# Attention stage: rotations moved behind the score maxima, the choice matmuls moved into a scores bank, both heads' turned probabilities copied at once

## The chip, the cores and the metric

One core of one Trainium2 chip runs one fused program. The metric is the device time of the whole program in microseconds (us). The engines work in parallel, each through its own list of instructions in order: TensorE (PE, whose weight loads are listed as PEld), VectorE (DVE), ScalarE (ACT), GpSimd (POOL) and SyncE (SP, which only starts transfers). They meet at semaphores, which the program sets and waits for by hand. No scheduler reorders anything: what stands in an engine's list is what that engine does next, and a wait holds up all that stands behind it on its engine.

## The reference

Three layers over x of 8 batches x 256 tokens x 128:

```python
    x = x + 0.5 * _L0_ffn_ref(_layernorm(x, axis=-1), ...)
    x = x + _L0_attn_ref(_layernorm(x, axis=-1), ...)
    x = x + 0.5 * _L0_ffn_ref(_layernorm(x, axis=-1), ...)
```

The first and third are the same mixture of 64 experts (each token's 8 best, and a shared one). The one between is attention, 16 heads of 64:

```python
        q = q * cos + rotate_half(q) * sin + fenc
        k = k * cos + rotate_half(k) * sin + fenc
        dots = jnp.einsum('bhid,bhjd->bhij', q, k) * scale
        attn = jax.nn.softmax(dots, axis=-1)
        out = jnp.einsum('bhij,bhjd->bhid', attn, v)
        out = out.transpose(0, 2, 1, 3).reshape(b, n, INNER)
        return out @ w_out.T + b_out
```

## The kernel before

The change is in `attention`, the middle stage. It works in units of one batch and one pair of heads: 8 batches (`BATCH`) x 8 pairs (`PAIRS`) = 64 units, u = 8b + p. Batches 2 to 6 run in a loop on most engines; the others are written out.

The steps of a unit are spread over several turns of the loop over p. In the turn (b, p) the engines work on different units at once:

- **Projections** `qkv` (L72, L73, L74: three matmuls for one product of split float32): q and k of unit u+3 (`AHEAD` = 3) into bank `QB`, six matmuls of 128x256; v of unit u+3 into the first half of bank `VB`, three matmuls.
- **Rotation** `rotate` on DVE (L2076 with cos, L2079 with sin): from `QB` into the buffers `m1` and `m2`. POOL adds the two (`add`, L1856, 128x512 float32, SBUF to SBUF). PE turns the sum (`turn`, L1947, and two matmuls of the Fourier part, L1952) and ACT copies it out (`take_qk`, L2257).
- **Scores** (`scores`, L1962) of unit u into banks `SB` and `SB+1`, one for each head. They contract over 64 rows, so the two heads use half the rows of the array each.
- **Softmax**: `maximum` on DVE (L2086) for each head, `exps` on ACT (L2263) with the sums of rows; `invert` on DVE (L2092, 128x2). Head 0 is normalised on DVE (`normalise`, L2098, two instructions of 128x256, SBUF to SBUF), head 1 on ACT (L2272).
- `turn_p` (L1974) transposes the probabilities of unit u-1, into banks `PB` and `PB+1`; ACT copies each head's (`take_p`, L2279) into `pT`. `values` (L1987) of unit u-2 (`VLAG` = 2), 64 columns of the array for each head, into the second half of `VB`; ACT copies that (`take_o`, L2284). `project` (L2002) of unit u-3 (`JLAG` = 3). `take_v` (L2246) copies v out of the first half of `VB`.

Bank `VB` is shared: `values` waits until v of unit u+2 has been copied out (`vev`), and the v product waits until the values of unit u-2 have been copied out (`oev`).

Beside this, DVE adds up the first layer's choices for a later batch (`choice`, L2108, two instructions a turn, both inputs in SBUF), makes the layer norm of the next batch (`stats`, `mean`, `apply`, `split`, `bias`), and does most of the choice of experts for the third layer from the batch that is done (`pick_...`). Three times a batch (p = 0, 5, 6) a choice step needs the array and a bank: `pick_ranks`, `pick_turn`, `pick_logits` write into `room`, the first half of `VB`, and ACT takes the result at the head of the turn. From batch 2 on POOL sends two indirect transfers (`dispatch`, L1181) each turn.

Of the kernel before, what the change touches and what calls it, by code (L numbers as in the profile page):

```python
# [26 lines left out]
P = 128  # L27
BATCH, SEQ, DIM = 8, 256, 128
# [1715 lines left out]
def attention(nc, x, wk, ydram, attn_w, ready_w, y01, y01_in, summed, s, ps, wg, tables, xs_dram, sents):  # L1744
# [10 lines left out]
    with ExitStack() as ctx:  # L1755
# [62 lines left out]
        LN_STATS, LN_MEAN, LN_APPLY, LN_BIAS = 0, 1, 2, 3  # L1818
# [5 lines left out]
        with nc.Block(no_gpsimd_drain=True) as block:  # L1824
# [14 lines left out]
            def _(pool):  # L1839
# [3 lines left out]
                def load_cur(b):  # L1843
                    after(pool, vp, PAIRS * b)
# [23 lines left out]
                def batch(b):  # L1868
                    last = b == BATCH - 1
                    for p in range(PAIRS):  # L1870
                        if there(b, p, -AHEAD, False, last):
                            add(*pair(b, p, AHEAD))
# [43 lines left out]
            def _(pe):  # L1916
                def qkv(b, p, xs):
# [6 lines left out]
                    mm.then_inc(qk, 1)  # L1924
                    taken = u - AHEAD - VLAG + 1
# [42 lines left out]
                def turn_p(b, p, h):  # L1968
                    u = PAIRS * b + p
                    pe.wait_ge(pn[h], u + 1)  # L1970
                    after(pe, pte, 2 * u + h - 1)
# [35 lines left out]
                def room(b, p):  # L2007
                    u = PAIRS * b + p
                    pe.wait_ge(vev, min(u + AHEAD, PAIRS * BATCH) if isinstance(u, int) else u + AHEAD)
                    pe.wait_ge(oev, u - VLAG)  # L2010
                    return ps[:, VB, 0:TPB * P]

                def batch(b, kind):
                    first, last = kind == FIRST, kind == LAST
                    for p in range(PAIRS):
                        scores(b, p)
                        if p == 0 and kind in (MIDDLE, LAST):
# [5 lines left out]
                        if there(b, p, -1, first, last):  # L2023
                            turn(*pair(b, p, 1))
                        if there(b, p, 1, first, last):
                            turn_p(*earlier(b, p, 1), 0)
                            turn_p(*earlier(b, p, 1), 1)
                        if p == 0 and kind in (MIDDLE, LAST):
                            pe.wait_ge(s.room_r, 3 * (b - 2) + 3)
                        if p == PICK_TURN and not first:  # L2030
                            pe.wait_ge(s.room_r, 3 * (b - 1) + 1)
                        if p == PICK_LOGITS and not first:
                            pe.wait_ge(s.room_r, 3 * (b - 1) + 2)
                        if there(b, p, VLAG, first, last):
                            values(*earlier(b, p, VLAG), last and p + AHEAD > PAIRS)
                        if p + AHEAD < PAIRS:
                            qkv(b, p + AHEAD, xcur)
                        elif not last:
                            if p + AHEAD == PAIRS:
                                pe.wait_ge(xx, b + 2)  # L2040
                            qkv(b + 1, p + AHEAD - PAIRS, xnext)
                        if there(b, p, JLAG, first, last):
                            project(*earlier(b, p, JLAG), not last, last and p + AHEAD >= PAIRS)
                        if p == LN_TURN and not last:
                            turn_x(b + 1, False)
# [5 lines left out]
                qkv(0, 0, xnext)  # L2051
                qkv(0, 1, xnext)
                turn(0, 0)
                qkv(0, 2, xnext)
# [17 lines left out]
            def _(v):  # L2072
# [80 lines left out]
                def split(b):  # L2153
                    v.wait_ge(xev, b + 1)
                    after(v, vp, PAIRS * (b - 1) + AHEAD)
# [20 lines left out]
                def batch(b, kind, more):  # L2176
                    first, last = kind == FIRST, kind == LAST
                    for p in range(PAIRS):
                        maximum(b, p, 0)
                        maximum(b, p, 1)  # L2180
                        if p == RES_AT and not first:
                            residual(b - 1)
                        invert(b, p, 0)
# [29 lines left out]
                        if there(b, p, -AHEAD, first, last):  # L2213
# [277 lines left out]
```

## Time and profile before

| | |
|---|---|
| median of three runs | 913.99 us (912.68 to 914.81) |
| the profiled execution | 914.71 us, of which the span from first to last instruction is 912.7 us |
| PE, PEld busy | 93%, 82% of the span |
| DVE, ACT, POOL busy | 62%, 55%, 54% |
| attention stage | from about 294 us to 663 us |

A span is read by stage. Outside the attention stage the program is the two expert layers, where other things bind, and where the change alters nothing. In the attention stage one turn of the loop takes some 5.6 to 5.9 us, and 64 of them stand one behind the other. So an edit that makes a turn 0.1 us longer or shorter is worth about 6 us. Each row of the chain of waits or of the timeline has the start (us from the span's start) and the length of what it lists.

### The profile page before, as it was taken

How to read it: one execution, taken by the hardware profiler on the slowest of the kernel's cores; microseconds unless marked ns; L12 is line 12 of the kernel's file. 1: busy time of each engine (PE TensorE's matmuls, PEld its weight loads, DVE VectorE, ACT ScalarE, POOL GpSimd, SP SyncE). 2: the span in 40 equal slices, each digit the busy share in tenths (PEclk: the TensorE clock that was granted, in tenths of full speed). 3: DMA queues.
4: the chain of work that ended last, by engine and by line, in shares of the span. 5: the costliest groups of instructions: out<-in, count | busy, mean ns of one | idle time of the engine just before them, and what ended most of it. 6: DMA issues, size and time to landing. Idle time of an engine off the chain costs nothing.

```text
span 912.7 us, 18913 instructions
## 1 busy us (share of the span) xinstructions
PE 850.9 (93%) x6328; PEld 745.5 (82%) x6328; DVE 568.5 (62%) x1736; ACT 503.8 (55%) x1376; POOL 494.3 (54%) x536
## 2 busy tenths in 40 slices
PE   5989989999964999999999999999979999999977
PEld 4889989999963777777777777777679999999962
DVE  7947753333336878888888888877543376433446
ACT  4423333333321888888888888888832333333336
POOL 4156777777762222256666666666657354444440
PEclk9779999999995999999999999999999999999999
DMA  9947877776626890000000000000050588888756
GB/s 327 368 160 225 258 231 227 236 242 218 205 87 227 197 151 1 1 14 27 23 25 25 25 25 25 22 19 15 6 211 18 182 313 284 279 287 291 241 190 259
DMA packets 65150, 140.70 MB, mean 154 GB/s; under 512 B 10223, under 2 KB 37296, under 8 KB 63940
## 3 DMA queue, kind: packets, MB, share of 16 engines
q1 hardware_dynamic: 53316, 118.59, 39.9%
q0 software_dynamic: 11776, 21.39, 7.5%
q8 instruction: 31, 0.51, 0.2%
q14 instruction: 27, 0.22, 0.1%
HBM read 107.72 MB, written 35.56 MB: 157 GB/s over the span
## 4 chain that ended last, share of the span: by engine, by line
PE 62%; POOL 13%; issue 6%; DVE 5%; ACT 4%; DMA 4%; DVEq 0%; ACTq 0%; POOLq 0%; SPq 0%
PE ps L1387 12%; PE ps L1962 6%; POOL y_rows L589 6%; POOL f_xg L578 6%; PE ps L1987 6%; PE ps L1406 6%; PE ps L615 5%; PE ps L1974 5%; PE ps L72 4%; PE ps L1947 3%; PE ps L2002 3%; PE ps L73 2%; PE ps L74 2%; ACT at_prob L2263 2%; PE ps L655 2%
## 5 line engine op out<-in xcount | busy, mean ns | idle before, releaser
L1856 POOL TENSOR_TENSOR at_m<-at_m 128x512 f32<-128x512 f32 x64 | 81.5, 1274 | 147.8 <-DVE at_m L2079 147.8
L1181 POOL DMA_INDIRECT xs_rows<-xr,slots_of x128 | 127.4, 995 | 43.8 <-issue 32.1
L2263 ACT ACTIVATE at_prob<-ps,at_nmax 128x256 f32<-128x256 f32 x256 | 118.0, 475 | 39.2 <-DVE at_nmax L2086 38.8
L1365 POOL DMA_INDIRECT y_rows<-f_og,f_put x80 | 81.7, 1021 | 95.6 <-ACT f_og L1518 76.1
L878 DVE TENSOR_TENSOR f_ehid<-f_esil,ps 128x480 f32<-128x480 f32 (+1 forms) x80 | 50.8, 634 | 116.0 <-ACT f_esil L719 107.9
L1657 DVE TENSOR_TENSOR f_hid<-f_sil,ps 128x480 f32<-128x480 f32 (+1 forms) x80 | 50.7, 634 | 107.0 <-ACT f_sil L1511 100.4
L1387 PE MATMUL ps<-f_xgT,f_ring 128*128 128x160 f32 x768 | 115.0, 299 | 1.7 <-issue 1.7
L615 PE MATMUL ps<-f_xgT,f_ring 128*128 128x160 f32 x768 | 114.9, 299 | 0.2 <-issue 0.2
L719 ACT ACTIVATE f_esil<-ps 128x480 f32<-128x480 f32 (+1 forms) x80 | 44.4, 555 | 120.8 <-PE ps L615 120.8
L1511 ACT ACTIVATE f_sil<-ps 128x480 f32<-128x480 f32 (+1 forms) x80 | 44.4, 555 | 118.8 <-PE ps L1387 118.8
L1387 PEld LDWEIGHTS ps<-f_xgT,f_ring 128*128 128x128 f32 x768 | 107.0, 190 | 2.1 <-issue 2.1
L615 PEld LDWEIGHTS ps<-f_xgT,f_ring 128*128 128x128 f32 x768 | 107.0, 190 | 0.3 <-issue 0.3
L578 POOL DMA_INDIRECT f_xg<-xn_rows,f_take x80 | 84.0, 1050 | 34.1 <-issue 34.1
L2086 DVE TENSOR_REDUCE at_nmax<-ps 128x2 f32<-128x512 f32 x128 | 82.3, 685 | 25.0 <-PE ps L1962 24.6
L589 POOL DMA_INDIRECT y_rows<-f_og,f_put x80 | 79.7, 996 | 33.0 <-issue 23.5
L1962 PE MATMUL ps<-at_qkT 64*128 64x256 f32 x512 | 72.9, 403 | 2.1 <-ACT at_qkT L2257 2.1
L2279 ACT COPY at_pT<-ps 128x512 f32<-128x512 f32 x128 | 70.9, 627 | 0.0
L1987 PE MATMUL ps<-at_pT,at_v 128*64 128x256 f32 x512 | 69.4, 392 | 0.9 <-ACT at_pT L2279 0.9
L1974 PE MATMUL ps<-ident,at_prob 128*128 128x128 f32 x512 | 66.8, 273 | 1.3 <-ACT at_pT L2279 0.7
L655 PE MATMUL ps<-f_ehid,f_ring 128*128 128x160 f32 x384 | 62.6, 299 | 0.0
L1406 PE MATMUL ps<-f_hid,f_ring 128*128 128x160 f32 x384 | 62.6, 299 | 0.0
L2272 ACT ACTIVATE at_prob<-at_prob,at_rinv 128x256 f32<-128x256 f32 x128 | 61.2, 552 | 0.1
(256 smaller groups left out, 1844.2 us busy)
## 6 DMA issues: line engine op xcount, KB each, us to landing
f_ring<-in_wexp SPq DMA_DIRECT2D x128, 576.0 KB, 4.6
y_rows<-zeros SPq DMA_DIRECT2D x16, 512.0 KB, 6.2
f_yt<-y_rows SPq DMA_DIRECT2D x4, 2048.0 KB, 8.5
at_yt<-y_rows SPq DMA_DIRECT2D x6, 1024.0 KB, 4.9
xs_rows<-at_blank SPq DMA_DIRECT2D x16, 342.5 KB, 10.0
f_xg<-xs_rows SPq DMA_DIRECT2D x16, 342.5 KB, 3.3
y_rows<-f_og,f_put POOLq DMA_INDIRECT x160, 2.7
y<-y_rows SPq DMA_DIRECT2D x4, 512.0 KB, 4.4
```

Source lines behind the costliest of these rows:

```text
L578: nc.gpsimd.indirect_dma_start(xg[:, G % SG, c, :], None, xn_dram, bass.IndirectOffsetOnAxis(take[:, n:n + 1], 0), bounds_check=last_token ...
L589: nc.gpsimd.indirect_dma_start(ydram, bass.IndirectOffsetOnAxis(put[:, n:n + 1], 0), og[:, G % SG, c, :], None, bounds_check=last_row, oob ...
L615: mm = nc.tensor.matmul(ps[:, HB + 2 * h + half, f * w:(f + 1) * w], weights[:, half * FFN + f * P:half * FFN + (f + 1) * P], moving, star ...
L1181: nc.gpsimd.indirect_dma_start(xs_dram, bass.IndirectOffsetOnAxis(s.slots_of[:, t, k:k + 1], 0), s.xr[:, t, :], None, bounds_check=last_sl ...
L1365: nc.gpsimd.indirect_dma_start(ydram, bass.IndirectOffsetOnAxis(put[:, n:n + 1], 0), og[:, g, c, :], None, bounds_check=last_row, oob_is_e ...
L1387: mm = nc.tensor.matmul(ps[:, HB + 2 * h + half, f * w:(f + 1) * w], weights[:, half * FFN + f * P:half * FFN + (f + 1) * P], moving, star ...
L1406: mm = nc.tensor.matmul(ps[:, OB, 0:CAPACITY], ring[:, GE * g + e, c], hid[:, e % 2, f * CAPACITY:(f + 1) * CAPACITY], start=(f == 0), sto ...
L1962: mm = nc.tensor.matmul(ps[:, SB + h, t * SEQ:(t + 1) * SEQ], qkT[r, p % 2, t * P:(t + 1) * P], qkT[r, p % 2, SEQ:], start=True, stop=True)
L1974: mm = nc.tensor.transpose(ps[:, PB + h, j * SEQ + t * P:j * SEQ + (t + 1) * P], prob[:, p % 2, h, t, j * P:(j + 1) * P], ident[:, :])
L1987: mm = nc.tensor.matmul(ps[h * DH:(h + 1) * DH, VB, SEQ:], vsb[:, p, j, h * DH:(h + 1) * DH], pT[:, p % 2, h, j, :], start=(j == 0), stop= ...
L2086: nc.vector.tensor_reduce(nmax[:, p % 2, h, :], ps[:, SB + h, :].rearrange("p (t k) -> p t k", t=TPB), AX.X, ALU.max, negate=True).then_in ...
L2263: mm = nc.scalar.activation(prob[:, p % 2, h, t, :], ps[:, SB + h, t * SEQ:(t + 1) * SEQ], ACT.Exp, bias=nmax[:, p % 2, h, t:t + 1], accum ...
```

## The change

Seven edits in one, all in `attention`:

1. DVE: `rotate` no longer ends a turn. It stands behind the two `maximum` (and behind `residual`), in front of `invert` and `normalise` of head 0, and it handles the q and k that were projected in the turn before, so unit u+2 in the turn of u.
2. POOL: `add` follows it, unit u+2 in the turn of u.
3. PE: the order of a turn is now scores, values, turn, turn_p, project, turn_x, v product, choice matmuls, q/k product. Before it was scores, choice matmuls, turn, turn_p, values, q/k product, v product, project, turn_x.
4. PE: the choice matmuls write into bank `SB`, after the first head's exponentials have read it, and the next turn's scores wait until ACT has read the result.
5. ACT: the order of a turn is now exps, take_o, take_qk, take_p, the copy of a choice step, normalise, take_v.
6. ACT: `take_p` copies both heads in one instruction of 128x1024; before, one of 128x512 for each.
7. DVE: `bias` moves from p = 3 to p = 5. Some waits name `qk` in place of `vp`, since the q/k product is now the later one.

```diff
                 def room(b, p):
                     u = PAIRS * b + p
-                    pe.wait_ge(vev, min(u + AHEAD, PAIRS * BATCH) if isinstance(u, int) else u + AHEAD)
-                    pe.wait_ge(oev, u - VLAG)
-                    return ps[:, VB, 0:TPB * P]
+                    pe.wait_ge(ex, 2 * u + 1)
+                    return ps[:, SB, 0:TPB * P]
...
+                        if p == PICK_TURN + 1 and not first:
+                            pe.wait_ge(s.room_r, 3 * (b - 1) + 1)
...
                         scores(b, p)
+                        if there(b, p, VLAG, first, last):
+                            values(*earlier(b, p, VLAG), ending)
+                        if there(b, p, -1, first, last):
+                            turn(*pair(b, p, 1))
+                        if there(b, p, 1, first, last):
+                            turn_p(*earlier(b, p, 1), 0, ending)
+                            turn_p(*earlier(b, p, 1), 1, ending)
+                        if there(b, p, JLAG, first, last):
+                            project(*earlier(b, p, JLAG), not last, not there_is_v)
...
+                            project_v(*nxt, xs)
...
+                        if there_is_v:
+                            project_qk(*nxt, xs)
...
                         maximum(b, p, 1)
                         if p == RES_AT and not first:
                             residual(b - 1)
+                        if there(b, p, 1 - AHEAD, first, last) and not (first and p == 0):
+                            rotate(*pair(b, p, AHEAD - 1))
                         invert(b, p, 0)
                         normalise(b, p, 0)
...
-                        if there(b, p, -AHEAD, first, last):
-                            rotate(*pair(b, p, AHEAD))
...
-                def take_p(b, p, h):
+                def take_p(b, p):
                     u = PAIRS * b + p
-                    act.wait_ge(pt, 2 * u + h + 1)
-                    nc.scalar.copy(pT[:, p % 2, h, :, :].rearrange("p j q -> p (j q)"), ps[:, PB + h, :]).then_inc(pte, 1)
+                    act.wait_ge(pt, 2 * u + 2)
+                    nc.scalar.copy(pT[:, p % 2, :, :, :].rearrange("p h j q -> p (h j q)"),
+                                   ps[:, PB:PB + 2, :].rearrange("p h c -> p (h c)")).then_inc(pte, 2)
```

The order of DVE in the turn p = 2 of the looped batches, before (at_m is `m1`/`m2`, at_nmax the maxima, at_prob the probabilities, at_yt the first layer's results):

```order
L2086 TENSOR_REDUCE at_nmax<-ps 128x2
L2092 RECIPROCAL at_rinv<-at_rsum 128x2
L2098 TENSOR_SCALAR at_prob<-at_prob,at_rinv 128x256 x2
L2105 REGISTER_ALU
L2108 ISA
L2108 SCALAR_TENSOR_TENSOR x<-at_yt,wk,x 128x128
L2108 ISA
L2108 SCALAR_TENSOR_TENSOR x<-at_yt,wk,x 128x128
L2092 RECIPROCAL at_rinv<-at_rsum 128x2
L2148 TENSOR_SCALAR at_xn<-x,at_mv,at_st 128x128 x2
L2076 TENSOR_TENSOR at_m<-ps,cos 128x512
L2079 TENSOR_TENSOR at_m<-ps,sin 128x512
```

and the same turn of the changed kernel, whose lines are numbered 9 higher here:

```order
L2095 TENSOR_REDUCE at_nmax<-ps 128x2
L2084 REGISTER_ALU
L2085 TENSOR_TENSOR at_m<-ps,cos 128x512
L2088 TENSOR_TENSOR at_m<-ps,sin 128x512
L2101 RECIPROCAL at_rinv<-at_rsum 128x2
L2107 TENSOR_SCALAR at_prob<-at_prob,at_rinv 128x256 x2
L2114 REGISTER_ALU
L2117 ISA
L2117 SCALAR_TENSOR_TENSOR x<-at_yt,wk,x 128x128
L2117 ISA
L2117 SCALAR_TENSOR_TENSOR x<-at_yt,wk,x 128x128
L2101 RECIPROCAL at_rinv<-at_rsum 128x2
```

The two rotations went from behind the turn's other work to a place directly ahead of the first RECIPROCAL and the normalising of head 0.

PE in the turn p = 3 of batch 1, before, from the scores to the first projection:

```order
L1962 MATMUL ps<-at_qkT 128x256 [waits at_qkev]
L1962 MATMUL ps<-at_qkT 128x256 x3
L1947 MATMUL ps<-ident,at_m 128x128 [waits at_msum]
L1947 MATMUL ps<-ident,at_m 128x128 x3
L1952 MATMUL ps<-ffs,wfs 128x256 x2
L1974 MATMUL ps<-ident,at_prob 128x128 [waits at_pte,at_pn0]
L1974 MATMUL ps<-ident,at_prob 128x128 x3
L1974 MATMUL ps<-ident,at_prob 128x128 [waits at_pte,at_pn1]
L1974 MATMUL ps<-ident,at_prob 128x128 x3
L1987 MATMUL ps<-at_pT,at_v 64x256 [waits at_vev]
L1987 MATMUL ps<-at_pT,at_v 64x256 x3
```

and of the changed kernel (L1965 are the scores, L1991 the values, L1950 and L1978 the two turns):

```order
L1965 MATMUL ps<-at_qkT 128x256 [waits at_qkev]
L1965 MATMUL ps<-at_qkT 128x256 x3
L1991 MATMUL ps<-at_pT,at_v 64x256 [waits at_vev]
L1991 MATMUL ps<-at_pT,at_v 64x256 x3
L1950 MATMUL ps<-ident,at_m 128x128 [waits at_msum]
L1950 MATMUL ps<-ident,at_m 128x128 x3
L1955 MATMUL ps<-ffs,wfs 128x256 x2
L1978 MATMUL ps<-ident,at_prob 128x128 [waits at_pn0]
L1978 MATMUL ps<-ident,at_prob 128x128 x3
L1978 MATMUL ps<-ident,at_prob 128x128 [waits at_pn1]
L1978 MATMUL ps<-ident,at_prob 128x128 x3
```

The values stand directly behind the scores now, with their wait for ACT's last copy of the turn before (`vev`), and all the rest of PE's turn stands behind that wait.

## Rows read from the trace of the kernel before

**Rows 1.** Busy time by stretch: PE, PEld, DVE, ACT, POOL, clock, DMA share, GB/s

```profile
450.00:500.00 50.00, 49.76 (x390) 38.48 (x387) 42.63 (x134) 43.22 (x138) 30.71 (x33) 1.00 0.07 25
```

**Rows 2.** The chain of waits in order of time over one turn: start, us, what

```profile
332.17 1.06 PE ps L1962 x8
333.24 0.59 PE ps L1947 x4
...
334.94 1.01 PE ps L1987 x8
335.95 0.32 PE ps L72
336.26 0.12 PE ps L73
...
336.85 0.26 PE ps L72
...
337.35 0.45 PE ps L2002 x4
```

**Rows 3.** The timeline of the same turn

```profile
331.87 0.68 DVE L2079 TENSOR_TENSOR at_m<-ps,sin 128x512 f32<-128x512 f32 x1
...
332.10 1.14 PE L1962 MATMUL ps<-at_qkT 64*128 64x256 f32 x8
332.64 1.27 POOL L1856 TENSOR_TENSOR at_m<-at_m 128x512 f32<-128x512 f32 x1 [3.80 <-DVE at_m L2079]
332.67 0.42 ACT L2246 COPY at_v<-ps 128x256 f32<-128x256 f32 x1
...
333.27 1.29 DVE L2086 TENSOR_REDUCE at_nmax<-ps 128x2 f32<-128x512 f32 x2 [0.71 <-PE ps L1962]
...
335.05 0.17 DVE L2092 RECIPROCAL at_rinv<-at_rsum 128x2 f32<-128x2 f32 x1 [0.49 <-ACT at_prob L2263]
335.25 0.62 DVE L2098 TENSOR_SCALAR at_prob<-at_prob,at_rinv 128x256 f32<-128x256 f32 x2
...
336.27 0.40 ACT L2284 COPY at_oTh<-ps 128x256 f32<-128x256 f32 x1
336.31 0.16 DVE L2092 RECIPROCAL at_rinv<-at_rsum 128x2 f32<-128x2 f32 x1
...
336.54 1.11 ACT L2279 COPY at_pT<-ps 128x512 f32<-128x512 f32 x2
...
337.50 0.96 ACT L2272 ACTIVATE at_prob<-at_prob,at_rinv 128x256 f32<-128x256 f32 x2
```

**Rows 4.** All of line 1937 (one per batch, two instructions each) from 400 to 592 us

```profile
L1937 PEld LDWEIGHTS ps<-ident,at_xn x10: 141/142/144, 406.0 to 590.7; 128*128 128x128 f32 x10
```

**Rows 5.** Line 2098, ns min/median/max: first 320 to 360 us, then 400 to 600

```profile
L2098 DVE TENSOR_SCALAR at_prob<-at_prob,at_rinv x14: 346/350/354, 324.0 to 358.0; 128x256 f32<-128x256 f32 x14
...
L2098 DVE TENSOR_SCALAR at_prob<-at_prob,at_rinv x69: 333/354/617, 403.7 to 599.8; 128x256 f32<-128x256 f32 x69
```

**Rows 6.** The timeline at 507 us, POOL and DVE

```profile
507.28 1.00 POOL L1181 DMA_INDIRECT xs_rows<-xr,slots_of  x1 [0.16 <-issue]
507.65 0.74 DVE L2098 TENSOR_SCALAR at_prob<-at_prob,at_rinv 128x256 f32<-128x256 f32 x2
```

**Rows 7.** POOL's groups of instructions by form, 400 to 600 us: count, busy us, mean ns

```profile
L1856 POOL TENSOR_TENSOR at_m<-at_m 128x512 f32<-128x512 f32 x35 | 44.6, 1275 | 55.6 <-DVE at_m L2079 55.5
...
L1847 POOL CAST at_xcur<-at_xnext 128x512 fp32r<-128x512 f32 x4 | 2.4, 612 | 0.0
L1063 POOL COPY xnT<-p_turned 128x256 f32<-128x256 f32 x4 | 1.6, 396 | 0.0
```

**Rows 8.** The timeline of PE at the end of the last batch, scores alone

```profile
642.02 1.13 PE L1962 MATMUL ps<-at_qkT 64*128 64x256 f32 x8
646.66 1.14 PE L1962 MATMUL ps<-at_qkT 64*128 64x256 f32 x8
651.53 0.70 PE L1962 MATMUL ps<-at_qkT 64*128 64x256 f32 x4
```

More of the change, by code:

```diff
@@ L1843, in load_cur @@
                 def load_cur(b):
-                    after(pool, vp, PAIRS * b)
+                    after(pool, qk, PAIRS * b)
                     pool.wait_ge(xx, b + 1)
@@ L1868, in batch @@
                 def batch(b):
-                    last = b == BATCH - 1
+                    first, last = b == 0, b == BATCH - 1
                     for p in range(PAIRS):
-                        if there(b, p, -AHEAD, False, last):
-                            add(*pair(b, p, AHEAD))
+                        if there(b, p, 1 - AHEAD, False, last) and not (first and p == 0):
+                            add(*pair(b, p, AHEAD - 1))
                         if p == LN_MEAN and not last:
@@ L1924, in qkv, with project_v @@
                     mm.then_inc(qk, 1)
+                def project_v(b, p, xs):
+                    u = PAIRS * b + p
                     taken = u - AHEAD - VLAG + 1
@@ L1966, in scores, with turn_p @@
                                 mm.then_inc(sc, 1)
-                def turn_p(b, p, h):
+                def turn_p(b, p, h, alone=True):
                     u = PAIRS * b + p
                     pe.wait_ge(pn[h], u + 1)
-                    after(pe, pte, 2 * u + h - 1)
+                    if alone:
+                        after(pe, pte, 2 * u + h - 1)
                     for t in range(TPB):
@@ L2015, in batch @@
                     for p in range(PAIRS):
-                        scores(b, p)
+                        ending = last and p + AHEAD > PAIRS
+                        there_is_v = p + AHEAD < PAIRS or not last
+                        nxt, xs = pair(b, p, AHEAD), xcur if p + AHEAD < PAIRS else xnext
+                        if p == 1 and kind in (MIDDLE, LAST):
+                            pe.wait_ge(s.room_r, 3 * (b - 2) + 3)
+                        if p == PICK_TURN + 1 and not first:
+                            pe.wait_ge(s.room_r, 3 * (b - 1) + 1)
+                        if p == PICK_LOGITS + 1 and not first:
+                            pe.wait_ge(s.room_r, 3 * (b - 1) + 2)
+                        scores(b, p)
+                        if there(b, p, VLAG, first, last):
[7 more added lines that the diff above has]
+                            project(*earlier(b, p, JLAG), not last, not there_is_v)
+                        if p == LN_TURN and not last:
+                            turn_x(b + 1, False)
+                        if there_is_v:
+                            if p + AHEAD == PAIRS:
+                                pe.wait_ge(xx, b + 2)
+                            project_v(*nxt, xs)
                         if p == 0 and kind in (MIDDLE, LAST):
@@ L2022, in batch @@
                             pick_logits(nc, pe, s, room(b, p), b - 1)
[L2023 to L2045, printed above, removed]
+                        if there_is_v:
+                            project_qk(*nxt, xs)
                         if p == PAIRS - 1 and not last:
@@ L2154, in split @@
                     v.wait_ge(xev, b + 1)
-                    after(v, vp, PAIRS * (b - 1) + AHEAD)
+                    after(v, qk, PAIRS * (b - 1) + AHEAD)
                     after(v, xc, b)
@@ L2324, in _ @@
                 take_o(BATCH - 1, PAIRS - 2)
-                for h in range(2):
-                    take_p(BATCH - 1, PAIRS - 1, h)
+                take_p(BATCH - 1, PAIRS - 1)
                 pick_take_ranks(nc, act, s, ps[:, QB, :], BATCH - 2)
```

32 lines of the change are left out of this document (17 added, 15 removed).

## The prediction

> **What bounds the kernel now.** I read the busy shares by stretch first. In the attention stage PE is busy 49.76 of 50 us at a granted clock of 1.00, the upper of its two levels, while DVE has 42.63 and ACT 43.22 [rows 1]. That could be an engine at its limit or an engine whose matmuls hide short waits, so the chain of waits comes next: over one turn it is PE alone, 5.63 us from the scores' start to the end of `project` (337.35 + 0.45 - 332.17), where the next scores start [rows 2]. Line 1937 runs once a batch, and in 184.7 us it comes back four times (406.0 to 590.7): 46.2 us a batch, 5.77 a turn [rows 4]. Eight bare turns are 45.0, the rest is turn_x and the three choice steps, and a few waits. So PE sets the stage, and what a turn costs on PE counts 60 times.
>
> The chain also shows what in PE's turn is not matmul. A 128x256 projection matmul in the midst of others takes 0.12 (336.26 to 336.85 are five of them); the first behind `values` has 0.32, so leaving the 64-column mode costs 0.20. The first of the v product has 0.26, so 0.14 is a wait: take_o ends at 336.67 (336.27 + 0.40) [rows 3], and the product stands behind it. Four transposes take 0.59 behind the scores, against 0.44 if each is a quarter of 0.45, the four matmuls of `project` [rows 2]: leaving the 64-row mode costs 0.15.
>
> **The change on PE alone.** Scores and values stand together, so one return to the full array goes: the 0.20 behind `values`, and the 0.15 behind it is the same as before behind the scores. The v product moves behind values, turn, turn_p and project, so its bank is read long before; the 0.14 goes too. That is 5.63 - 0.34 = 5.29 for a turn of PE, 4.23 of it from the start of `values` on (5.29 - 1.06). No row shows the way from scores to values without something between; I take it as free, and its bounds are 0 and another 0.20.
>
> **What PE waits for next.** `values` now comes 1.06 into the turn and waits for `take_v`, ACT's last copy of the turn before. ACT's chain from the scores' start: take_v ends at 333.09 (332.67 + 0.42), 0.99 after the scores of the next turn start by the timeline (332.10) [rows 3] and so 6.62 after its own scores. PE sees it a little later, which makes about 6.67. The single copy of 128x1024 in place of two that take 1.11 together [rows 3] saves little: the bounds are 0 and 0.1, I take 0.02, which leaves 6.65. So `values` of a turn start no earlier than 6.65 after the scores of the turn before, and the next scores 4.23 later. Two turns take 10.88: 5.44 a turn, if DVE does its part in time. That would be a gain of 0.19 a turn.
>
> **Does DVE?** From the scores' start at 332.10, the maxima start at 1.17 and last 1.29 [rows 3]. Today the RECIPROCAL then waits for ACT's exponentials 0.49, the normalising of head 0 starts 0.20 later, and the second RECIPROCAL 1.06 after that (336.31 - 335.25); ACT normalises head 1 at 5.40 (337.50) [rows 3]. After the change: two maxima and two rotations at a pace of 0.61, the last ending at 1.17 + 3 x 0.61 + 0.68 = 3.68; RECIPROCAL at 3.59, normalising at 3.79, second RECIPROCAL at 4.85, done at 5.01. That is 0.4 ahead of ACT. By time alone the move is free.
>
> But it puts two things side by side that never met before. POOL's `add` starts 0.09 after the rotation ends (331.87 + 0.68 = 332.55, and 332.64) and lasts 1.27 [rows 3]. Today the maxima, which read PSUM, run beside it. In the changed kernel it starts at 3.77 and DVE's two normalising instructions, SBUF to SBUF, at 3.79: they meet in every turn. What does such a meeting cost? Where POOL does nothing else, from 320 to 360 us, the normalising instruction takes 346 to 354 ns, all 14 of them; from 400 on, where POOL issues indirect transfers, it goes up to 617 [rows 5]. At 507 the pair takes 0.74 in place of 0.62, and ends 0.11 after the transfer's instruction (508.39 against 508.28) [rows 3, 6]. So DVE is stopped until POOL is through, and then runs at its usual pace. For the add I need the part of 1.27 in which it holds its operands. A cast of 512 columns takes 0.612 and a copy of 256 takes 0.396 [rows 7]: 0.84 ns a column and 0.18 fixed. The add's moving part is then 1.27 - 0.18 = 1.09. If the first normalising instruction ends 0.11 after the add, it ends at 5.15 where it would have ended at 4.14 (3.79 + 0.35): DVE is 1.0 late. Bounds: nothing, if DVE gets all its instructions in ahead of POOL, and 1.27. The longest stop that a row shows is 617 - 350 = 0.27, from a transfer that takes 1.00. The add moves far more data, so I take 1.0. If DVE wins the race with its first instruction, its second or the two `choice` instructions behind it (two SBUF inputs) would be stopped instead, which comes to the same.
>
> The Trainium skill, "SBUF — State Buffer", section "Who interferes with whom", has a rule for this: VectorE and GpSimd share a port pair, whoever issues first holds it for the whole instruction and the other "fully blocks", and `tensor_scalar` in its two-port mode and instructions with two SBUF inputs both need it. By that rule the stop is 1.0 to 1.27 in each turn, and the forecast slower; without it the sum would be 0.19 a turn to the good. The trace agrees as far as it goes, since 0.27 is a stop of just this kind [rows 5].
>
> **The sum.** With DVE 1.0 late, the second RECIPROCAL is done at 6.01 and ACT normalises head 1 at about 6.07, against 5.38: 0.69 late, all of it passed on to take_v and to PE's values. 6.65 + 0.69 = 7.34, plus 4.23 is 11.57 for two turns: 5.79 a turn, 0.16 more than 5.63. In the batches with choices DVE itself comes near the limit: 42.63 of 50 [rows 1] is 4.92 of a turn of 5.77, and with 1.0 more, less 0.1 for the stops by transfers that go away (transfers follow the add and then fall on maxima), 5.8 of work in a turn. It is uneven (norms, choice of experts), so the maxima will start late in some turns, and that delays the same chain. PE's extras (46.2 - 45.0 = 1.2 a batch) put the other chain at 5.94. I take 6.05, 0.28 more than 5.77, for the four batches 2 to 5 with the full DVE load; the estimate of 0.11 for unevenness is my choice. 32 x 0.28 = 9.0. Of the other 32 turns, 28 at 0.16 give 4.5. At the end of the last batch PE has no projections, and two turns take 4.64 and 4.87 [rows 8]; now the next scores wait there until ACT has taken the choice result behind its copies, so each is about 5.8: 2.1. Together 15.6. The third layer starts when attention ends, and its weights are loaded from then on, so it is shifted whole.
>
> 914.7 (profiled execution) + 15.6 = 930.3; the median is 0.7 lower than the profiled execution, so 929.6, rounded to 929.
>
> **Rivals.** *A: slower by the stop, 70%.* As above. Its own range: a stop of 0.8 gives 5.69 a turn by the same sum, and little unevenness, about +5; one of 1.27 and more unevenness gives about +24. 919 to 938.
>
> *B: no stop, 20%, the rival on the other side.* If POOL's add waits until DVE's normalising and `choice` are through, nothing of DVE is late, and the add has time: PE turns unit u+2 only 2.1 into the next turn, at 7.5, and the add would end by 6.2. Then 5.44 a turn: 0.19 x 60 = 11.4, less 2.1 at the end and less 0.2 a batch at p = 5, where the scores wait for ACT's copy of the choice result: about -8, 906. It speaks for it that most normalising instructions beside a transfer run unslowed (median 354) [rows 5]; against it, that those beside the transfer's holding part do not. It decides at a stop of 0.3, where ACT first notices.
>
> *C: a short stop, 10%.* If the add holds its operands only for about 0.6, ACT's normalising is 0.3 late and a turn takes 5.59, with DVE's unevenness about the old pace: 910 to 918.
>
> **How the numbers follow.** The predicted time is A's. The range leaves out the upper tail of A and the best of B: 906 to 937. A difference of 0.2% (1.8 us) is what a measurement of this kernel can tell from none. Slower by more: A and a third of C, 0.73. Within: 0.05. Faster: B and a part of C, 0.22.
>
> **What would show it.** Right: in the timeline of the changed kernel the normalising instruction at 1.2 to 1.4 us, ending 0.1 after POOL's add, in nearly each turn; PE waiting for take_v before `values`; turns of 5.8 in batch 0 and about 6 later; the wait for take_o at the v product gone. DVE's busy time up by some 50 us though it has the same work. Wrong: normalising at 0.35 and the add at 1.6 or more (rival B), or a turn at 5.3 on PE. The prediction is also wrong if the way from scores to values costs more than I gave it; by the two-turn sum each 0.1 there adds only 0.05 a turn.

## The result: 2.45% slower, and the profile of the changed kernel

The changed kernel takes 937.0 us (935.7 to 937.7, four runs), the kernel before 914.4 in the same session: ratio 1.0245, 95% interval 1.022 to 1.0269. The forecast was 929 with a range of 906 to 937. The direction and the mechanism came as forecast; the size was 22.6 us where 15.6 had been worked out, and 937.0 is the very end of the range. Of the runs further down, e2 and e11 each had one execution of four, 1411 and 1433 us long, at a granted clock of 0.56 and 0.63, and no ratio uses it.

The view of busy time by stretch, changed kernel, the stretch of [rows 1] (span, PE, PEld, DVE, ACT, POOL, clock, DMA share, GB/s):

```profile
450.00:500.00 50.00, 44.24 (x356) 35.14 (x356) 47.38 (x120) 39.22 (x119) 29.76 (x31) 1.00 0.07 23
```

PE has fallen from 49.76 to 44.24 and DVE has risen from 42.63 to 47.38, at the same granted clock of 1.00: PE now waits, and DVE is the engine near its limit. DVE has no more work than before. The normalising instruction, first from 320 to 360 us and then from 400 to 600 (ns min/median/max), against [rows 5]:

```profile
L2107 DVE TENSOR_SCALAR at_prob<-at_prob,at_rinv x14: 340/1045/1409, 320.7 to 356.5; 128x256 f32<-128x256 f32 x14
...
L2107 DVE TENSOR_SCALAR at_prob<-at_prob,at_rinv x63: 340/1398/2175, 404.2 to 598.7; 128x256 f32<-128x256 f32 x63
```

It took 346 to 354 in the first of these stretches before. Now about half of them, the first of each pair, take 1.40, which is a stop of 1.05; the others keep their 0.34. The chain of waits of two bare turns in batches 0 and 1 (start, us, what), to be held against [rows 2]:

```profile
334.58 1.11 PE ps L1965 x8
335.69 1.27 DVE at_nmax L2095 x2
336.96 0.60 DVE at_m L2085
337.56 0.60 DVE at_m L2088
...
338.26 1.67 DVE at_prob L2107 x2
339.93 0.52 DVE x L2117 x2
340.45 0.09 DVE at_rinv L2101
...
340.56 0.91 ACT at_prob L2281 x2
341.47 0.26 ACT at_v L2255
...
341.78 1.08 PE ps L1991 x8
```

Before, this chain was PE alone. Now it leaves PE behind the scores, goes through all of DVE's turn, with 1.67 in it where the same two instructions took 0.62, then through ACT's normalising and `take_v`, and comes back to PE at `values`. The timeline around that place, with three scores starts in a row:

```profile
334.51 1.13 PE L1965 MATMUL ps<-at_qkT 64*128 64x256 f32 x8
...
338.24 1.28 POOL L1856 TENSOR_TENSOR at_m<-at_m 128x512 f32<-128x512 f32 x1 [4.79 <-DVE at_m L2088]
338.26 1.67 DVE L2107 TENSOR_SCALAR at_prob<-at_prob,at_rinv 128x256 f32<-128x256 f32 x2
...
339.94 1.13 PE L1965 MATMUL ps<-at_qkT 64*128 64x256 f32 x8
...
341.78 1.08 PE L1991 MATMUL ps<-at_pT,at_v 128*64 128x256 f32 x8 [0.71 <-ACT at_v L2255]
...
346.01 1.13 PE L1965 MATMUL ps<-at_qkT 64*128 64x256 f32 x8
```

POOL's add starts 0.02 ahead of the normalising. It takes no longer than before (1.28 against 1.27), and DVE is through 0.41 after it (338.24 + 1.28 = 339.52 and 338.26 + 1.67 = 339.93): the last bit of the first instruction, and the second. `values` waits 0.71 for `take_v` and starts 7.27 after the scores of the turn before (341.78 - 334.51; the forecast had 7.34), and the next scores 4.23 after that. Two turns take 11.50 (346.01 - 334.51), 5.75 each; over the eight turns from 311.18 to 357.52 it is 5.79, which was the forecast.

In the batches with choices it is worse. The line that runs once a batch, to be held against [rows 4]:

```profile
L1940 PEld LDWEIGHTS ps<-ident,at_xn x10: 139/142/144, 411.5 to 610.9; 128*128 128x128 f32 x10
```

Four batches take 199.4, 49.85 each and 6.23 a turn, where it was 5.77 and the forecast 6.05. The timeline of POOL and DVE in one of these turns shows why:

```profile
451.06 0.72 POOL L1851 TENSOR_TENSOR at_st<-at_st,at_pexp 128x2 f32<-128x2 f32 x1 [1.44 <-DVE at_st L2151]
...
454.33 0.98 POOL L1181 DMA_INDIRECT xs_rows<-xr,slots_of  x1 [0.30 <-issue]
...
454.64 2.48 DVE L2107 TENSOR_SCALAR at_prob<-at_prob,at_rinv 128x256 f32<-128x256 f32 x2
455.32 1.31 POOL L1856 TENSOR_TENSOR at_m<-at_m 128x512 f32<-128x512 f32 x1
```

Here the add is late behind a transfer, and the normalising starts in the transfer. It is stopped first by that and then by the add, which follows at once: 2.48 in place of 0.62. The add is late because POOL too works its list in order: in the turn before it has a step of a layer norm, which waits for DVE's statistics (1.44 idle at 451.06), and the two transfers stand behind that. The double stop happens at p = 2 and, at 467.17 with 2.27, at p = 4 in each of the four batches, and the turns that follow take 7.12 and 7.14 (scores starts):

```profile
456.29 1.13 PE L1965 MATMUL ps<-at_qkT 64*128 64x256 f32 x8
463.41 1.13 PE L1965 MATMUL ps<-at_qkT 64*128 64x256 f32 x8
468.82 1.13 PE L1965 MATMUL ps<-at_qkT 64*128 64x256 f32 x8
475.96 1.13 PE L1965 MATMUL ps<-at_qkT 64*128 64x256 f32 x8
```

At the end of the last batch, against [rows 8], the scores wait for the copy of a choice result out of their own bank. The two turns take 6.12 and 5.70 in place of 4.64 and 4.87, 2.3 more (forecast 2.1):

```profile
663.50 1.13 PE L1965 MATMUL ps<-at_qkT 64*128 64x256 f32 x8
669.62 1.13 PE L1965 MATMUL ps<-at_qkT 64*128 64x256 f32 x8 [0.77 <-ACT p_turned L1051]
675.32 1.14 PE L1965 MATMUL ps<-at_qkT 64*128 64x256 f32 x8 [1.02 <-ACT p_logits L1089]
```

So the 22.4 by which the span grew (935.1 - 912.7) are 14.7 in the four loaded batches (199.4 - 184.7), 2.3 at the end and 5.4 in all the rest. That rest is not the other turns alone: the first scores start 1.1 later (295.66 against 294.57), the third layer's first matmuls 23.7 later (687.70 against 664.03), and the third layer takes 1.3 of that back.

### The profile page after: what moved, and what is told of

The parts are those of the page before. It is cut to its first block, busy times and chain, and to the rows that moved or that the text cites. A ratio compares the mean times of both kernels' runs of the same rounds, so it can differ in the third digit from the quotient of the medians.

```text
span 935.1 us, 18791 instructions
## 1 busy us (share of the span) xinstructions
PE 839.5 (90%) x6328; PEld 744.9 (80%) x6328; DVE 629.7 (67%) x1736; ACT 504.9 (54%) x1312; POOL 497.3 (53%) x536
## 4 chain that ended last, share of the span: by engine, by line
PE 53%; DVE 19%; issue 9%; POOL 5%; ACT 4%; DMA 3%; DVEq 1%; ACTq 0%; POOLq 0%; SPq 0%
PE ps L1387 12%; PE ps L615 11%; PE ps L1406 5%; DVE at_nmax L2095 4%; PE ps L655 4%; DVE at_prob L2107 3%; PE ps L1965 3%; PE ps L1991 3%; DVE at_m L2085 3%; DVE at_m L2088 3%; PE ps L1978 2%; POOL y_rows L589 2%; POOL f_xg L578 2%; DVE x L2117 2%; ACT at_prob L2281 2%
## 5 line engine op out<-in xcount | busy, mean ns | idle before, releaser
L1181 POOL DMA_INDIRECT xs_rows<-xr,slots_of x128 | 129.3, 1010 | 42.3 <-issue 32.0
L2107 DVE TENSOR_SCALAR at_prob<-at_prob,at_rinv 128x256 f32<-128x256 f32 x128 | 115.2, 939 | 2.3
L1991 PE MATMUL ps<-at_pT,at_v 128*64 128x256 f32 x512 | 69.4, 392 | 33.8 <-ACT at_v L2255 32.6
L1991 PEld LDWEIGHTS ps<-at_pT,at_v 128*64 128x64 f32 x512 | 31.1, 136 | 67.3 <-ACT at_v L2255 56.1
L1965 PE MATMUL ps<-at_qkT 64*128 64x256 f32 x512 | 72.6, 402 | 3.9 <-ACT at_qkT L2266 1.5
L2281 ACT ACTIVATE at_prob<-at_prob,at_rinv 128x256 f32<-128x256 f32 x128 | 58.1, 502 | 32.1 <-DVE at_rinv L2101 31.3
L2288 ACT COPY at_pT<-ps 128x1024 f32<-128x1024 f32 x64 | 67.0, 1046 | 2.7 <-PE ps L1978 2.2
L1978 PE MATMUL ps<-ident,at_prob 128*128 128x128 f32 x512 | 66.6, 273 | 1.6 <-ACT at_pT L2288 1.5
```

The costliest lines, as they stand in the source:

```text
L1181: nc.gpsimd.indirect_dma_start(xs_dram, bass.IndirectOffsetOnAxis(s.slots_of[:, t, k:k + 1], 0), s.xr[:, t, :], None, bounds_check=last_sl ...
L1965: mm = nc.tensor.matmul(ps[:, SB + h, t * SEQ:(t + 1) * SEQ], qkT[r, p % 2, t * P:(t + 1) * P], qkT[r, p % 2, SEQ:], start=True, stop=True)
L1978: mm = nc.tensor.transpose(ps[:, PB + h, j * SEQ + t * P:j * SEQ + (t + 1) * P], prob[:, p % 2, h, t, j * P:(j + 1) * P], ident[:, :])
L1991: mm = nc.tensor.matmul(ps[h * DH:(h + 1) * DH, VB, SEQ:], vsb[:, p, j, h * DH:(h + 1) * DH], pT[:, p % 2, h, j, :], start=(j == 0), stop= ...
L2107: mm = nc.vector.tensor_scalar(prob[:, p % 2, h, t, :], prob[:, p % 2, h, t, :], rinv[:, p % 2, h, t:t + 1], None, ALU.mult)
```

## The experiments

Ten kernels. "A batch" is a quarter of the time from the first to the last of the rows of the line that runs once a batch (`turn_x`), as above. Each row of the table was compared with the kernel before on its own chip (913.6 to 914.4 us).

| kernel | us | ratio, 95% interval | a batch |
|---|---|---|---|
| before | 914.0 | 1 | 46.2 |
| the changed kernel | 937.0 | 1.0245 (1.022 to 1.0269) | 49.9 |
| e1 changed, add late | 914.3 | 1.0008 (0.9996 to 1.002) | 46.6 |
| e2 before, add late | 940.7 | 1.0291 (1.0272 to 1.031) | 50.8 |
| e3 before, rotations moved | 938.8 | 1.026 (1.0242 to 1.0279) | 51.1 |
| e4 changed, old rotation | 920.7 | 1.0081 (1.0062 to 1.0099) | 47.3 |
| e5 changed, add beside the maxima | 906.7 | 0.9911 (0.9895 to 0.9927) | 44.8 |
| e6 e5, choice in bank VB | 907.5 | 0.9937 (0.9921 to 0.9954) | 45.4 |
| e7 changed, add in halves | 932.3 | 1.0198 (1.0181 to 1.0215) | 49.2 |
| e9 e5, `take_v` early | 905.5 | 0.9911 (0.9895 to 0.9928) | 44.6 |
| e10 e9, `take_o` early | 899.8 | 0.9851 (0.9835 to 0.9868) | 44.2 |
| e11 changed, `turn` behind | 936.9 | 1.0257 (1.0236 to 1.0277) | 49.9 |

### The add held back in the changed kernel

```diff
+                def add(b, p, behind=None):
                     pool.wait_ge(rope, u + 1)
+                    if behind is not None:
+                        pool.wait_ge(rc, 2 * behind + 2)
...
-                            add(*pair(b, p, AHEAD - 1))
+                            add(*pair(b, p, AHEAD - 1), PAIRS * b + p)
```

> The changed kernel with one wait more: POOL's add of the rotated halves waits until DVE has inverted both heads' sums of the same turn, so it can't meet DVE's normalising or choice instructions. Nothing else differs and no work is left out. Theory 1 (the stop of DVE beside POOL's add is what costs): the normalising instruction is back at 0.35 us, a turn of batch 0 takes about 5.45, a batch with choices 45 to 46 us, the whole 905 to 911 us. Theory 2 (the order on PE costs: values directly behind the scores wait for ACT's last copy, whatever DVE does): the stop goes but the whole stays above 928 us.

Measured: 914.3 us, 23 less than the changed kernel. The normalising instruction is back at its own pace:

```profile
L2109 DVE TENSOR_SCALAR at_prob<-at_prob,at_rinv x68: 345/353/551, 403.5 to 595.4; 128x256 f32<-128x256 f32 x68
```

So one wait of POOL's, which adds no work and takes none away, gives back all that the change cost. But the 906 that the prediction gave this case, and the 905 to 911 expected here, did not come. The timeline of e1 at 457 us says why:

```profile
457.22 0.27 DVE L2168 TENSOR_SCALAR at_xtop<-at_xnew 128x256 int32<-128x256 int32 x1
457.45 1.26 POOL L1858 TENSOR_TENSOR at_m<-at_m 128x512 f32<-128x512 f32 x1 [0.86 <-DVE at_rinv L2103]
457.52 1.34 DVE L2171 CAST at_xnext<-at_xtop 128x256 fp32r<-128x256 f32 x1
```

The add no longer meets the normalising; it meets whatever DVE does next. All five casts of L2171 take 1.345 or more, where none took over 0.295 before. The smallest such instruction, 128x2, which takes 0.17 undisturbed, is stopped as long as a large one:

```profile
L2153 DVE TENSOR_SCALAR at_st<-at_mv x4: 1272/1274/1279, 440.0 to 579.5; 128x2 f32<-128x2 f32 x4
```

The stop had been moved, not removed.

### The add held back in the kernel before

```diff
+                    if behind is not None:
+                        pool.wait_ge(ex, 2 * behind + 1)
...
-                            add(*pair(b, p, AHEAD))
+                            add(*pair(b, p, AHEAD), PAIRS * b + p + 1)
```

> The kernel before with one wait more: POOL's add waits for the exponentials of head 0 of the next turn, so that it starts together with DVE's normalising, in the old order of all engines. Theory 1: the first normalising instruction goes from 0.35 to 1.3 to 1.5 us in nearly every turn; turns without choices stay near 5.63, since the old order leaves ACT's normalising and PE some 1 us of room; batches with choices, where DVE works 4.9 of 5.77 us a turn, go up to 48 to 50 us; the whole 925 to 935 us. Theory 2: POOL and DVE run beside each other, normalising at 0.35 us, the whole within 2 us of the kernel before.

Measured: 940.7, above the 925 to 935 expected. The kernel before can be made as slow as the changed one, or slower, by letting the two meet (from 400 to 600 us):

```profile
L2100 DVE TENSOR_SCALAR at_prob<-at_prob,at_rinv x62: 340/1014/1352, 403.7 to 595.9; 128x256 f32<-128x256 f32 x62
```

This run holds the add back as well, so it is not the stop alone. Around the start of batch 1 three turns in a row still take 5.62 or 5.63 (scores at 327.20, 332.82, 338.45 and 344.06) although the pair takes 1.95, 1.61 and 1.59 in them: the old order has slack for the stop there, though not in every turn (the one before takes 6.14). The loaded batches haven't, and go from 46.2 to 50.8.

### The rotations moved, alone, and everything else, alone

```diff
+                        if there(b, p, 1 - AHEAD, first, last) and not (first and p == 0):
+                            rotate(*pair(b, p, AHEAD - 1))
                         invert(b, p, 0)
...
-                        if there(b, p, -AHEAD, first, last):
-                            rotate(*pair(b, p, AHEAD))
```

> The kernel before with the DVE and POOL part of the change alone: rotate and add of unit u+2 directly behind the maxima; PE's and ACT's order, banks and copies as before. Theory 1: the stop is there (normalising at 1.4 us), turns of batch 0 stay at 5.63, batches with choices are bound by DVE at 49 to 50 us, the whole 925 to 932 us. Theory 2: PE's order is untouched, so the whole is within 3 us of the kernel before.

The other run is the changed kernel with just these lines, and POOL's for the add, as they were:

> The changed kernel with rotate and add back at the end of the turn (unit u+3), PE's and ACT's order as changed. Now DVE waits at the end of its turn for the q/k product, which is PE's last. Theory 1: no stop (normalising at 0.35 us, save beside transfers), maxima some 0.1 to 0.3 us later, the whole 906 to 918 us. Theory 2: above 928 us.

Measured: 938.8 and 920.7, both a few us above what was expected (925 to 932, and 906 to 918). The move of the rotations with its add costs 24.8 alone, as much as the whole change, and without it the rest costs 6.7. The rotations alone show the normalising at 340/1392/2154 ns (400 to 600 us). In the bare turns that costs nothing, as expected: seven of them take 5.62 each (scores from 313.79 to 353.12), where the changed kernel has 5.8, although the pair takes 1.67 or more in them. So there the stop costs only together with the new order of PE and ACT, in which `values` need `take_v` early; the loss of e3 is in the loaded batches, 51.1 us each. One reservation: there the q/k product, which the old order has early in PE's turn, also waits for the rotation to leave its bank (waits from 400 to 600 us, total, times, longest):

```profile
PEld ps L72 <- DVE at_m L2079: 15.6, 21, 1.1
```

so not all of the 24.8 is the stop. In e4 no normalising instruction loses more than 0.13 (345/353/481 ns), and its 6.7 are waits of another kind (400 to 600 us):

```profile
ACT at_prob L2272 <- DVE at_nmax L2095: 36.0, 34, 1.9
...
PEld ps L1991 <- ACT at_v L2255: 13.8, 34, 0.5
...
PEld ps L72 <- ACT at_oTh L2294: 8.9, 15, 1.1
```

With the rotations at the turn's end the maxima come late, ACT starts late, and PE, whose new order asks for `take_v` and `take_o` early, waits for both.

### The add beside the maxima

PE needs the sum early in its turn, so `turn` goes behind `turn_p` to give the add time.

```diff
+                    if behind is not None:
+                        pool.wait_ge(sc, 2 * behind + 3)
...
-                        if there(b, p, -1, first, last):
-                            turn(*pair(b, p, 1))
                         if there(b, p, 1, first, last):
                             turn_p(*earlier(b, p, 1), 0, ending)
                             turn_p(*earlier(b, p, 1), 1, ending)
+                        if there(b, p, -1, first, last):
+                            turn(*pair(b, p, 1))
```

> The changed kernel with POOL's add held back until the next unit's first scores are there, so that it runs beside DVE's maxima and rotations, which read PSUM; PE does turn_p ahead of turn, to give the add time. Theory 1: only the stop makes the changed kernel slow, and in the run with the late add it was not gone but had moved to DVE's later SBUF steps (the cast for x 1.34 in place of 0.29, the 128x2 step of the mean 1.27, the choice base 1.15). Then no DVE instruction is stopped beyond 0.3, a plain turn stays at 5.41, and batches 2 to 5 fall from 46.9 to about 45.0 us each, the others by about 1 to 1.5: about 905 us (903 to 908), 7 to 11 below the late add. Theory 2: the choice turns are slow because rotations ahead of normalise or the choice result in a scores bank hold the chain: 912 to 915, and turns of 6.7 at p = 5 stay. Theory 3: the rotations, with one input in SBUF, are stopped too: L2087 or L2090 at 1.3 or more in each turn, 925 to 935.

Measured: 906.7, 30 less than the changed kernel and 0.9% faster than before. The timeline of one turn:

```profile
332.49 1.13 PE L1967 MATMUL ps<-at_qkT 64*128 64x256 f32 x8
...
333.65 1.29 DVE L2097 TENSOR_REDUCE at_nmax<-ps 128x2 f32<-128x512 f32 x2 [1.61 <-PE ps L1967]
333.70 0.63 PEld L1993 LDWEIGHTS ps<-at_pT,at_v 128*64 128x64 f32 x8 [0.48 <-ACT at_v L2257]
...
333.76 1.27 POOL L1858 TENSOR_TENSOR at_m<-at_m 128x512 f32<-128x512 f32 x1 [3.58 <-PE ps L1967]
...
336.24 0.62 DVE L2109 TENSOR_SCALAR at_prob<-at_prob,at_rinv 128x256 f32<-128x256 f32 x2
...
337.93 1.13 PE L1967 MATMUL ps<-at_qkT 64*128 64x256 f32 x8
```

Add and maxima run side by side, neither slower for it (1.27 and 1.29, the two of [rows 3]), and the normalising stands at 0.62. Over the loaded batches the 72 maxima take 673 to 692 ns and the 36 first rotations, whose first 0.2 lie beside the add, 673 to 682. The Trainium skill, "SBUF — State Buffer", section "Who interferes with whom", says that a VectorE instruction "with at most one SBUF input, outside the 2-port perf modes, does not contend with GpSimd"; the trace agrees for the maxima in full, and for the rotations (one input in PSUM, one in SBUF) only as far as these 0.2 reach.

A turn takes 5.44 (337.93 - 332.49), and in it `values` waits for `take_v`. That is the prediction's two-turn chain without the stop: `values` at 339.13 are 6.64 after the scores of the turn before, where 6.65 had been worked out.

The control has PE's new order alone, with the add where the change has it.

> A control: the changed kernel with only PE's turn behind turn_p, and the add where the change has it, beside DVE's normalising. Theory 1 (the stop is the cause): the stop is still 1.05 in each turn, 935 to 939, and no part of the gain of the run with the add beside the maxima comes from PE's order. Rival: PE's order gives part of the 30 us: 920 to 930.

Measured: 936.9. The stop is as before (340/1048/2162 ns from 400 to 600 us), and nothing of the 30 us came from PE's order.

### The add in two halves

```diff
-                    nc.gpsimd.tensor_tensor(m1[:, p % 2, :], m1[:, p % 2, :], m2[:, p % 2, :],
-                                            ALU.add).then_inc(msum, 1)
+                    for half in range(2):
+                        c = slice(half * TPB * QKW // 2, (half + 1) * TPB * QKW // 2)
+                        mm = nc.gpsimd.tensor_tensor(m1[:, p % 2, c], m1[:, p % 2, c], m2[:, p % 2, c], ALU.add)
+                    mm.then_inc(msum, 1)
```

> The changed kernel with POOL's add as two instructions of 128x256 one behind the other, nothing else. Theory 1: DVE is held for the whole of one POOL instruction and gets in when that one ends. The normalising instruction then takes about 0.35 + 0.55 in the first half and perhaps a part again beside the second: the first at about 0.9, the whole 920 to 930 us, clearly below 937. Theory 2: the lock isn't by the instruction but by how much POOL moves in all: two halves stop DVE for 1.0 again, plus POOL's fixed 0.18, 936 to 941. Rival to both: if the stop doesn't matter, 937 whatever the mean of the normalising instruction.

Measured: 932.3, between the two expectations, and only half of either is right. The timeline, and all normalising instructions from 320 to 360 us:

```profile
331.20 1.47 POOL L1858 TENSOR_TENSOR at_m<-at_m 128x256 f32<-128x256 f32 x2 [3.61 <-DVE at_m L2090]
331.23 1.59 DVE L2109 TENSOR_SCALAR at_prob<-at_prob,at_rinv 128x256 f32<-128x256 f32 x2
```

```profile
L2109 DVE TENSOR_SCALAR at_prob<-at_prob,at_rinv x14: 815/837/856, 319.8 to 354.9; 128x256 f32<-128x256 f32 x14
```

DVE does get in when one POOL instruction ends: none of these waits for both halves. But POOL's second half starts too and stops DVE's second instruction, so each is stopped for 0.49 (837 - 350) and the pair takes 1.59 where it was 1.67. In these turns the stop goes by the instructions that overlap, one for one; cutting one side up shares it out.

### The choice results back in bank VB

```diff
                 def room(b, p):
                     u = PAIRS * b + p
-                    pe.wait_ge(ex, 2 * u + 1)
-                    return ps[:, SB, 0:TPB * P]
+                    pe.wait_ge(vev, min(u + AHEAD, PAIRS * BATCH) if isinstance(u, int) else u + AHEAD)
+                    pe.wait_ge(oev, u - VLAG)
+                    return ps[:, VB, 0:TPB * P]
...
+                        scores(b, p)
...
+                        if p == PICK_TURN and not first:
+                            pick_turn(nc, pe, s, room(b, p), b - 1)
...
+                        if chosen and there(b, p, 1, first, last):
+                            turn_p(*earlier(b, p, 1), 0, ending)
```

> The run before this one (add beside the maxima), and the choice matmuls back in bank VB behind the scores, their copy back at the head of ACT's turn, turn_p between them and the values in these turns. Theory 1: what remains of the choice steps' cost is the next scores' wait for ACT's copy out of bank SB: the two turns at the end of the last batch fall from about 5.8 to about 5.0 or less each, p = 6 of each batch by 0.1 to 0.3 and p = 5 too: 2 to 4 us less than that run, about 902. Theory 2: the choice matmuls wait for take_v at the head and hold the values behind them, which is the critical chain: the same or up to 2 us more than that run.

Measured: 907.5, no difference from e5 that these runs can tell. Each theory was right in its place. At the end of the last batch two turns fall from 5.86 and 5.71 to 5.04 and 5.12 (starts of the scores 633.75, 639.61, 645.32 in e5; 635.08, 640.12, 645.24 here), 1.4 less. In the loaded batches the choice holds up the values behind it: 45.35 a batch against 44.8.

### What holds the turn at 5.44

```diff
                         exps(b, p, 0)
-                        exps(b, p, 1)
                         if there(b, p, VLAG, first, last):
                             take_o(*earlier(b, p, VLAG))
+                        exps(b, p, 1)
...
-                        normalise(b, p, 1)
                         if there(b, p, -AHEAD, first, last):
                             take_v(*pair(b, p, AHEAD))
+                        normalise(b, p, 1)
```

First with `take_v` ahead of the normalising alone (the second hunk), then with both.

> The run with the add beside the maxima, and on ACT take_v ahead of head 1's normalising, nothing else. The question is what holds its turn at 5.44 where PE's own work was counted at 5.29. Theory 1 (the two-turn chain of the prediction): values waits 0.47 for take_v; with take_v about 0.96 earlier that wait goes, and the next thing in the way is take_o, which ends as the v product is due: 5.40 a turn, about 2 us less, 905. Theory 2: nothing else is in the way and PE comes down to 5.29 at once: 897 to 900. Rival: head 1's normalising ends 0.4 later and turn_p waits for it: no gain, 907 to 912.

> The run before this one (take_v ahead of the normalising), and on ACT take_o between the exponentials of head 0 and those of head 1. Theory 1: take_o is the last wait in PE's turn; without it a plain turn is 5.29 of PE alone and 60 turns give 6 to 9 us: 897 to 901. Rival: head 1's exponentials end 0.38 later, DVE's second RECIPROCAL and what stands behind it wait, the maxima of the loaded turns come late: 904 to 909. If the v product's wait for take_o was never real, it is the same as the run before it.

Measured: 905.5 and 899.8. With `take_v` early the wait of `values` is gone and a turn takes 5.41 (scores at 336.85 and 342.26), since the v product now stands behind `take_o`. In the whole that is too little to tell from e5: both have the ratio 0.9911. The two turns:

```profile
335.14 0.39 ACT L2296 COPY at_oTh<-ps 128x256 f32<-128x256 f32 x1
335.58 0.39 PE L72 MATMUL ps<-wqkv_high,at_xnext 128*128 128x256 f32 x1
...
340.55 0.38 ACT L2296 COPY at_oTh<-ps 128x256 f32<-128x256 f32 x1
340.99 0.39 PE L72 MATMUL ps<-wqkv_high,at_xcur 128*128 128x256 f32 x1
```

Each product starts 0.05 or 0.06 after the copy ends. With `take_o` early too, the chain of waits is PE alone again, over the whole turn, and the scores start every 5.29:

```profile
334.78 1.06 PE ps L1967 x8
335.85 1.01 PE ps L1993 x8
336.86 1.02 PE ps L1980 x8
```

```profile
334.71 1.14 PE L1967 MATMUL ps<-at_qkT 64*128 64x256 f32 x8
340.00 1.13 PE L1967 MATMUL ps<-at_qkT 64*128 64x256 f32 x8
345.30 1.13 PE L1967 MATMUL ps<-at_qkT 64*128 64x256 f32 x8
```

That is the 5.63 - 0.34 of the prediction. This kernel is the fastest of the study, 1.5% faster than before.

## Why the prediction was right, and where it was off

**PE's own turn, 5.29: right.** e10 shows it. The way from scores to values, which no row had shown, is free (334.78 + 1.06 = 335.84, values at 335.85).

**"The 0.14 goes too": wrong.** The prediction let the v product's wait for `take_o` vanish because the product moves back in PE's turn. But `take_o` stands behind all exponentials in both orders, and the product moved to just the moment when it ends. e9 and e10 show the wait: 5.41 with it, 5.29 without. It did not touch the forecast for the changed kernel, where `values` waits longer than that.

**The two-turn chain: right.** 5.44 without a stop was worked out from ACT's rows, and e5 has 5.44.

**The meeting and its price: right.** 1.0 was forecast for the stop and 1.05 measured; `values` at 7.34 and measured at 7.27; a bare turn at 5.79 and measured at 5.75 in the pair shown, 5.79 over eight turns. That the meeting is the cause is shown from both sides: e1 and e5 keep all of DVE's move and take the meeting away, for 23 and 30 us; e11 changes PE's order and keeps it, for nothing. In the size there was some luck. [rows 6] do not show that DVE is stopped until POOL is through: that pair starts 0.63 before the transfer ends and loses only 0.12. For the add the reading came true: the first instruction ends 0.14 after it (338.26 + 1.40 against 339.52).

**The loaded batches: the term that was mis-sized.** The prediction took 6.05 a turn, 5.94 and "the estimate of 0.11 for unevenness", and it measured 6.23, so the 0.11 would have had to be 0.29: 32 x 0.18 is 5.8 of the 7.0 us that were missing. Under it lies a step whose reason was wrong, "less 0.1 for the stops by transfers that go away". DVE's busy time in the four batches rose from 154.98 to 188.90 us, 1.06 a turn, where 1.0 less 0.1 had been taken. The transfers' stops did not go away where the add itself is late: a transfer and the add then stand back to back on POOL and DVE loses to both. Against the 1.67 of a plain meeting, the 2.48 at p = 2 and the 2.27 at p = 4 are 1.4 more a batch, 5.6 in four batches. That is the size of what was missing, and DVE, busy for 188.9 of 199.4 us, has little to take it up with; but no run took away the double stops and kept the plain ones. Outside these batches the growth was 5.4 against 4.5, and 2.3 against 2.1 at the end. These errors all go one way, and together they bring the time to the last value of the range. The number forecast is itself 0.6 below its own sum: 929.6 was rounded to 929.

**Rival B: its price was wrong.** It said that an add behind DVE's normalising would give 906. The add so placed gave 914.3, since DVE has more SBUF work behind it in the turns with a layer norm or a choice step. That 906.7 came with the add beside instructions that read PSUM is the same number for another kernel. A late place has to be free of a victim for the add's full 1.27, not only past the one that was looked at.

**Open.** How much of e3's 24.8 is the stop, and how much the q/k product's wait, was not separated. What the merged copy of the probabilities and the later `bias` are worth by themselves was not run. What the two remaining choice turns of a batch could give with another bank was not tried; e10 still has 44.2 a batch where eight bare turns are 42.3.

## What to carry to other kernels

Before an instruction of VectorE or GpSimd is moved, list what it will run beside on the other of the two, and what that reads: the neighbours that cost nothing here read PSUM, and those from SBUF to SBUF that it met cost nearly all that was left of the GpSimd instruction. If a reorder that ought to gain loses, look in the groups of instructions for one whose mean has risen while its count has not; a single wait on the other engine may turn the loss into the gain that was meant. And when a wait is said to vanish because the waiter moves, work out when the thing waited for will then be ready.

## What the runs showed of the hardware

- The stop does not depend on the size of the stopped instruction: in e1, 128x2 took 1.27 beside an add of 1.27, and a cast of 128x256 took 1.34. It goes by what is left of the add, less 0.1 to 0.2: with 1.24 left 128x2 lost 1.10 (its own time is 0.17), with 1.19 left the cast lost 1.05, and in the changed kernel, with 1.26 left, the normalising lost 1.05.
- A transfer's instruction on GpSimd and an add directly behind it act as one long stop: a single normalising instruction of the changed kernel took up to 2.18 in place of 0.35. In the kernel before, where the add never meets it, none lost more than 0.27.
- GpSimd gives way far less. Over the attention stage of the changed kernel the add takes 1267/1278/1442 ns (min/median/max of 59). By the Trainium skill, "SBUF — State Buffer", section "Who interferes with whom", whoever issues first holds the ports and the other blocks; the longest add, 1.44 at 303.95, is that of a turn in which VectorE's pair started 0.05 ahead of it. The trace agrees in the order, not in the size: VectorE's first instruction kept its 0.35, GpSimd lost 0.17 of the 0.30 that were left of it, and VectorE still took 1.64 for its pair, since its second instruction then lost to the add.
- Two ScalarE copies out of PSUM gain little by being merged: one of 128x1024 over two banks takes 1.01 to 1.06, and two of 128x512 took 1.11.
